# Second product of the expert paths: the last path's rounded rows packed beside their remainder, 14 products a tile for 15

## What is computed

```python
x_mixed = _mix(x, mix_kernel)
h = jnp.einsum('bsd,pdm->bspm', x_mixed, W1) + b1            # 9 paths, 64 wide each
stacked_paths = jnp.einsum('bspm,pmd->bspd', h, W2) + b2     # back to 256
scores = jnp.tanh(x_mixed @ Wo1 + bo1) @ Wo2 + bo2
weights = jax.nn.one_hot(jnp.argmax(scores, axis=-1), 9)
collapsed = jnp.einsum('bspd,bsp->bsd', stacked_paths, weights)
return _layernorm(x + collapsed, gamma, beta)
```

## Time and profile before

| what | us |
|---|---|
| median of three runs | 334.41 (333.69 to 335.15) |
| the profiled execution, its own time | 333.89 |
| its span, first to last instruction | 332.1 |

### The profile page before, as it was taken

The page is one execution under the profiler, slowest core; times in us unless marked ns, Lnnn a source line. Parts: engine busy times, 40 slices in busy tenths (PEclk is TensorE's granted clock), DMA queues, the critical chain, the costliest instruction groups (busy, mean ns, idle before and its releaser), DMA issues. The chain is left out here.

```text
span 332.1 us, 7164 instructions
## 1 busy us (share of the span) xinstructions
PE 301.6 (91%) x2764; PEld 227.6 (69%) x2764; DVE 265.0 (80%) x612; ACT 182.1 (55%) x282; POOL 218.5 (66%) x259
## 2 busy tenths in 40 slices
PE   1687899789999999999999999999999999999991
PEld 1564376365668767796779766796779677967890
DVE  2776799998779796989789796989399768695876
ACT  1364906734971677547852777357553655266620
POOL 0292065683296499966996499957886598629454
PEclk9999779999999999999999999999999999999996
DMA  8952020020002001200120010000100010001003
GB/s 227 221 106 80 2 79 3 0 82 0 3 12 69 2 0 65 80 2 3 65 73 8 0 54 14 1 2 0 65 2 1 3 64 2 2 0 65 0 3 126
DMA packets 20588, 13.16 MB, mean 40 GB/s; under 512 B 10114, under 2 KB 20427, under 8 KB 20555
## 3 DMA queue, kind: packets, MB, share of 16 engines
q1 hardware_dynamic: 18914, 12.14, 12.7%
q10 hardware_dynamic: 1640, 0.57, 0.8%
HBM read 8.51 MB, written 4.19 MB: 38 GB/s over the span
## 5 line engine op out<-in xcount | busy, mean ns | idle before, releaser
L1521 POOL TENSOR_TENSOR rs<-ve,halfneg 128x4 f32<-128x4 f32 x22 | 23.7, 1075 | 43.8 <-DVE ve L1164 43.8
L907 ACT ACTIVATE e<-ps 128x1024 f32<-128x1024 f32 x32 | 31.1, 1024 | 14.1 <-PE ps L584 14.1
L1201 DVE TENSOR_REDUCE mx<-ps 128x16 f32<-128x1024 f32 x32 | 38.0, 1216 | 0.3 <-PE ps L547 0.3
L1615 POOL TENSOR_TENSOR hml<-hs,hmh 128x512 fp32r<-128x512 f32 x28 | 35.0, 1280 | 4.4 <-ACT hmh L969 4.4
L709 PE MATMUL ps<-w2h,hmh 128*128 128x256 f32 (+1 forms) x140 | 35.0, 288 | 0.0
L710 PE MATMUL ps<-w2l,hmh 128*128 128x256 f32 (+1 forms) x140 | 34.1, 280 | 0.0
L620 PE MATMUL ps<-wo,osb 128*128 128x256 f32 x128 | 32.4, 400 | 0.2 <-DVE osb L1228 0.2
L1321 DVE TENSOR_TENSOR hs<-hs,ps 128x512 f32<-128x512 f32 x28 | 18.5, 682 | 16.6 <-PE ps L689 16.6
L1580 POOL TENSOR_TENSOR y<-xh2f,gms 128x256 f32<-128x256 f32 x24 | 20.4, 880 | 16.2 <-DVE xh2f L1173 16.2
L1546 POOL TENSOR_TENSOR x<-xin,bos 128x256 f32<-128x256 f32 x32 | 22.8, 745 | 11.0 <-DVE rDs L1219 10.3
L932 ACT ACTIVATE xh<-x,vb,rs 128x256 f32<-128x256 f32 x22 | 11.5, 591 | 31.5 <-POOL vb L1534 31.5
(11 more groups left out here) (174 smaller groups left out, 800.3 us busy)
## 6 DMA issues: line engine op xcount, KB each, us to landing
xin<-in_x SPq DMA_DIRECT2D x8, 512.0 KB, 3.9
out<-y SPq DMA_DIRECT2D x6, 512.0 KB, 2.9
min_<-in_mask_Bx1xSxS_ik SPq DMA_DIRECT2D x8, 128.0 KB, 3.9
hs<-in_L_ffn_W SPq DMA_DIRECT2D x2, 288.0 KB
hs<-in_L_ffn_W SPq DMA_DIRECT2D x1, 512.0 KB
out<-y SPq DMA_DIRECT2D x2, 256.0 KB, 2.1
out<-xin SPq DMA_DIRECT2D x2, 256.0 KB, 2.3
cst<-in_constants SPq DMA_DIRECT2D x1, 384.0 KB, 6.3
```

The costliest lines, as they stand in the source:

```text
L907: nc.scalar.activation(e[:, 2 * i:2 * i + 2, :], ps[:, bank:bank + 2, :], ACT.Exp).then_inc(s_e, 1)
L1201: v.tensor_reduce(mx[:, k, :].rearrange("p (a h) -> p a h", a=2), ps[:, bank:bank + 2, :].rearrange("p a (h s) -> p a h s", s=SK), AX.X, A ...
L1521: g.tensor_tensor(ln[7][:, :], ln[6][:, :], halfneg[:, :], ALU.pow).then_inc(s_r, 1)
L1615: g.tensor_tensor(L.lo(m, r), L.selected(m, r), L.hi(m, r).bitcast(F32), ALU.subtract).then_inc(L.s_hl, 1)
```

## The change

`m` = 4 is packed differently. The rounded rows of path 8 (64 partitions) are written a second time, to the 64 partitions below the remainder (`hi_below`, on ACT), and `w2h` carries W2[8] twice, one below the other. The one product lo x w2h of m = 4 then uses all 128 partitions and gives lo x w2h plus hi x w2h, so that hi x w2h of its own (L709 for m = 4) falls away: 14 products a tile. b2 leaves `w2h`; its rounded part and its remainder stand one below the other in `w2l` (18 rows below path 8's 64), and the one-hot row is written twice side by side, so that `rep(4)` makes 18 rows of it instead of 64. The setup loads W2[8] and b2 twice and makes b2's two parts with two DVE operations; a memset of `oh` goes.

```diff
-        oh = sb("oh", [P, NT, DM], BF16)
+        oh = sb("oh", [P, NT, 2 * NPATH], BF16)
...
+            def hi_below(self):
+                return hml[DM:, NM - 1, :]
...
         def rows_of(m):
-            return P if m < 4 else DM + NPATH
+            return P if m < 4 else DM + 2 * NPATH
+        def lo_rows_of(m):
+            return P if m < 4 else DM
...
                 load(w2_32[0:DM, 4, :], W2[8], s_wf)
-                load(w2_32[DM:DM + NPATH, 4, :], b2, s_wf)
+                load(w2_32[DM:, 4, :], W2[8], s_wf)
+                for i in range(2):
+                    load(y[DM + i * NPATH:DM + (i + 1) * NPATH, 1, :], b2, s_wf)
...
-                            mm = nc.tensor.matmul(o[DM:, ks], oh[:, k, :], ident_b,
-                                                  start=True, stop=True)
+                            mm = nc.tensor.matmul(o[DM:DM + 2 * NPATH, ks], oh[:, k, :], ident_b, start=True, stop=True)
...
-                        nc.tensor.matmul(o, L.hi(m, r)[:, ks], w2h[0:r, m, :], start=(m == 0), stop=False)
+                        if m < 4:
+                            nc.tensor.matmul(o, L.hi(m, r)[:, ks], w2h[:, m, :], start=(m == 0), stop=False)
                         nc.tensor.matmul(o, L.hi(m, r)[:, ks], w2l[0:r, m, :], start=False, stop=False)
                     else:
                         if k == 0:
                             pe.wait_ge(L.s_hl, L.first + L.count(b, j, NM, m + 1))
-                        mm = nc.tensor.matmul(o, L.lo(m, r)[:, ks], w2h[0:r, m, :], start=False, stop=(m == NM - 1))
+                            if m == NM - 1:
+                                pe.wait_ge(L.s_hb, L.count(b, j, 1, 1))
+                        mm = nc.tensor.matmul(o, L.lo(m, P)[:, ks], w2h[:, m, :], start=False, stop=(m == NM - 1))
...
                 nc.scalar.activation(L.hi(m, r), L.selected(m, r), ACT.Copy).then_inc(L.s_hh, 1)
+                if m == NM - 1:
+                    nc.scalar.activation(L.hi_below(), L.selected(m, DM), ACT.Copy).then_inc(L.s_hb, 1)
...
-                v.memset(oh[:, :, :], 0.0)
...
-                v.tensor_tensor(w2l[0:r, 4, :], w2_32[0:r, 4, :], w2h[0:r, 4, :].bitcast(F32),
-                                ALU.subtract).then_inc(s_w2l, 1)
+                v.tensor_tensor(w2l[0:DM, 4, :], w2_32[0:DM, 4, :], w2h[0:DM, 4, :].bitcast(F32), ALU.subtract)
+                b2_parts = w2l[DM:DM + 2 * NPATH, 4, :]
+                v.tensor_copy(b2_parts, b2_32).then_inc(s_b2h, 1)
+                dve.wait_ge(s_b2h, 1)
+                v.scalar_tensor_tensor(out=b2_parts, in0=b2_parts.bitcast(F32), scalar=cst[DM:DM + 2 * NPATH, C_LB:C_LB + 1],
+                                       in1=b2_32, op0=ALU.mult, op1=ALU.add).then_inc(s_w2l, 1)
...
-                v.tensor_tensor(oh[:, :, 0:NPATH], iota, per_tile(gidx), ALU.is_equal).then_inc(s_oh, 1)
+                twice = [P, NT, 2, NPATH]
+                v.tensor_tensor(oh[:, :, :].rearrange("p k (a n) -> p k a n", a=2),
+                                cst[:, C_IO:C_IO + NPATH].rearrange("p (k a n) -> p k a n", k=1, a=1).broadcast_to(twice),
+                                gidx[:, :].rearrange("p (k a n) -> p k a n", a=1, n=1).broadcast_to(twice),
+                                ALU.is_equal).then_inc(s_oh, 1)
```

More of the change, by code:

```diff
@@ L58 @@
 C_LO = C_IO + NPATH
-C_CST = C_LO + 1
+C_LB = C_LO + 1
+C_CST = C_LB + 1
 C_BC = C_CST
@@ L92, in constants @@
     c[:, C_LO:C_LO + 1] = np.where(r % 32 < 16, 0, -1)
+    c[:, C_LB:C_LB + 1] = np.where(r < DM + NPATH, 0, -1)
     c[:, C_IO:C_IO + NPATH] = np.arange(NPATH) - NPATH
@@ L190, in layer_program @@
         bc32 = y[:, 0, :].rearrange("p (c n) -> p c n", c=KD)
+        b2_32 = y[DM:DM + 2 * NPATH, 1, :]
         ps = stack.enter_context(nc.psum_tensor("ps", [P, 8, CH], F32))
@@ L247, in layer_program @@
         s_lf, s_lfa, s_lfv = sem("last_ffn_filled"), sem("last_ffn_read_by_act"), sem("last_ffn_read_by_dve")
+        s_hb, s_lhb, s_b2h = sem("last_path_hi_below_lo"), sem("last_chunk_last_path_hi_below_lo"), sem("b2_hi")
         s_lhh, s_lhl, s_lones = sem("last_selected_hi"), sem("last_selected_lo"), sem("last_b2_selector_ones")
@@ L283, in layer_program, with __init__ @@
         class Path:
-            def __init__(self, filled, read_by_act, read_by_dve, hi_done, lo_done):
+            def __init__(self, filled, read_by_act, read_by_dve, hi_done, lo_done, hi_below):
                 self.s_f, self.s_fa, self.s_fv, self.s_hh, self.s_hl = filled, read_by_act, read_by_dve, hi_done, lo_done
+                self.s_hb = hi_below
             def filled(self, b, j, use):
@@ L356, in lo, with hi_below @@
                 return qr[0:r, m, :] if m < KD else lhl[0:r, m - KD, :] if m < 4 else xTl[0:r, 0, :]
+            def hi_below(self):
+                return xTl[DM:, 0, :]
             def x(self, k):
@@ L362, in x @@
                 return ps[:, self.banks[("w2a", "w2b", "w2c")[group]], i * D:(i + 1) * D]
-        usual, last = Usual(s_f, s_fa, s_fv, s_hh, s_hl), Last(s_lf, s_lfa, s_lfv, s_lhh, s_lhl)
-        behind = BehindSteps(s_f, s_fa, s_fv, s_hh, s_hl)
+        usual, last = Usual(s_f, s_fa, s_fv, s_hh, s_hl, s_hb), Last(s_lf, s_lfa, s_lfv, s_lhh, s_lhl, s_lhb)
+        behind = BehindSteps(s_f, s_fa, s_fv, s_hh, s_hl, s_hb)
         last_y = xin[:, 1]
         def rows_of(m):
-            return P if m < 4 else DM + NPATH
+            return P if m < 4 else DM + 2 * NPATH
+        def lo_rows_of(m):
+            return P if m < 4 else DM
         block = stack.enter_context(nc.Block())
@@ L866, in split_ffn_weights @@
                 nc.scalar.activation(w2h[:, 0:4, :], w2_32[:, 0:4, :], ACT.Copy)
-                r = DM + NPATH
-                nc.scalar.activation(w2h[0:r, 4, :], w2_32[0:r, 4, :], ACT.Copy).then_inc(s_w2h, 1)
+                nc.scalar.activation(w2h[:, 4, :], w2_32[:, 4, :], ACT.Copy).then_inc(s_w2h, 1)
             def mask_copy(b, j, mask_bank):
@@ L1324, in last_selected_lo @@
             def last_selected_lo(b, j, m):
-                r = rows_of(m)
+                r = lo_rows_of(m)
                 dve.wait_ge(s_lhh, m + 1)
@@ L1699 @@
 WK_LOADS = 4
-WF_LOADS = KD + 1 + 4 + 3 + 4
+WF_LOADS = KD + 1 + 6 + 3 + 4
 _PREFIX = ("L0_xattn_", "L0_ffn_")
```

## The result

| | before | after |
|---|---|---|
| time, median of 4 runs | 334.77 us (333.69 to 335.15) | 338.44 us (336.87 to 339.32) |
| profiled execution, own time | 333.89 us | 338.51 us |
| its span | 332.1 us | 336.7 us |

The ratio of the times is 1.011, with a 95% interval of 1.0064 to 1.0155: slower by 1.1%, 3.7 us between the medians. The forecast was 338.0. The two profiled executions stand 4.6 us apart, a little more than the medians, and these 4.6 are what the traces have to account for.

A forecast was written before the change was run, and what follows sets the result against it. PE was taken to bound the kernel from about 75 us on. `rep(4)` +7.4 and removed products -3.8 gave +3.6 us: 333.89 profiled became 337.5, plus 0.5 for the median 338.0, range 335.8 to 340.6.

The forecast's parts named there:

- What bounds the kernel: From about 75 us to the end PE sets the time; an edit counts by its effect on distances between PE starts.
- The removal: In the w2 tiles, one 256-column product fewer a tile: 32 x 0.119 = 3.8 us less on PE.
- The cover at L631: PE's wait for the second layer norm: 0.86 us of cover before the change, still 0.5 after it.
- The 0.12 that DVE was said to have in hand: DVE's multiplication for m = 4 started 0.12 us after the last mask product, so the chain is later by only 0.81.
- 8 steps of 0.16: In `rep(4)`, alternating widths make eight steps, 1.28 us for 0.35: 0.93 more a chunk, 7.4 us in all.
- The estimate from the 128 cycles: In `rep(4)`, a drain of about 0.053 us a switch: a step of 0.11, 4.6 us in all, sum +0.8.
- Copy, remainder, setup: Added work on ACT, POOL and DVE's setup, and loads on SP: all hidden; uncovered, the copy would cost 0.63 a chunk.
- the copy delay ACT's L959 by about 0.1: In the tail, the copy delays L959 by about 0.1 us, hidden because `rep(4)` makes PE later by 0.93.
- The sum: Whole kernel: +7.4 - 3.8 = +3.6 us, with ends of +1.4 and +6.2.
- The two widths pass each other: Rival: in `rep(4)` the two widths run side by side without a switch, it stays at 0.35, 330.6 us; chance 0.12.
- A light switch: Rival: in `rep(4)` alternating costs half a switch, a step of 0.11, sum +0.4, 334.8 us; chance 0.07.
- The layer norm chain: Rival: the chain grows beyond its 0.5 cover, PE waits at L631 in five steps, 2 us more, 340.0; chance 0.08.

The follow-up runs named there:

- e1: The changed kernel with the second product of `rep(4)` made 36 columns wide instead of 18; 332.06 us, 0.9935 of before.
- e2: The changed kernel with that second product 64 columns wide and the memset of `oh` in setup again; 331.90 us, 0.9922 of before.
- e3: The changed kernel with `rep(4)` reordered, the four 64-wide products first, then the four 18-wide; 334.28 us, 0.9992 of before.
- e7: The changed kernel with `rep(4)` ordered 64, 18, 18, 64, 64, 18, 18, 64; 336.88 us, 1.0083 of before.
- e4: The kernel before with only the second half of `rep(4)` cut to 18 columns, 15 products a tile kept; 342.0 us, 1.0218 of before.
- e6: e2 with ACT's copy for chunk 7 moved behind the hidden rows of chunk 8 in the tail; 331.24 us, 0.9910 of before.
- e8: e6 with `scores_for_max(front, 2)` issued ahead of `rep(3)` instead of between `rep(3)` and `rep(4)`; 331.22 us, 0.9897 of before.
- e11: The changed kernel with one tiny one-column memset more on DVE in setup; 338.91 us (2 runs), 1.0128 of before.
- e5: e1 with the copy on ACT issued twice, the second waiting for the first; 332.4 us, 0.9940 of before.

## Why the prediction was right, and where it was not

- **What bounds the kernel**: PE's distance between starts, held. Every edit's worth could be read off the chunk: 0.48 predicted as 0.45.
- **The removal**, 0.119 us a product, 3.8 in all: right in the steady chunks (e1: 0.49 a chunk) and in the last w2 section. The full 3.8 never reached the end in a kernel without the narrow product: e2 has 2.65. The step that was too optimistic is the cover at L631: 0.86 was read from one steady chunk, the last step has none, and there the whole 0.48 of the gain goes. In the kernel after this hardly mattered, since `rep(4)` gave PE more time than was removed.
- **The cover at L631 in the steady chunk**, 0.5 foretold: measured 0.38 (ACT ends at 111.46, L650 starts at 111.84). The 0.12 that DVE was said to have in hand is not in hand. Its multiplication for m = 4 starts 0.11 behind the end of the masks in the kernel after too (102.56 behind 102.45), so the whole delay went into the chain and the cover shrank by the whole 0.48 of the removal.
- **`rep(4)`**, 8 steps of 0.16, 1.28 us: measured 1.30, with steps of 0.172 and 0.154. e3 and e7 show that most of it goes with the number of changes, at 0.10 to 0.11 each, and e4 that it is the width alone. The rule of the Trainium skill, TensorEngine Tiling (Array Packing), Key Properties, is that a change of tiling mode drains the engine. These traces agree in that every change has its price, also between two parts that share no column; that the price is a drain they do not show. The estimate from the 128 cycles of the Trainium skill, TensorE: Matmul & The Clock Gate, Step-by-step: what each phase is for (a step of 0.11, sum +0.8), was too low: the rows' 0.09 to 0.12 were the better source.
- **Copy, remainder, setup**: hidden in the steady chunks and in DVE's setup, as said; the loads ahead of 28 us are not decided. DVE's idle time ahead of its first reciprocal was 1.32 and is 0.77 with the added work. In the tail I had the copy delay ACT's L959 by about 0.1, and PE later by 0.93. The first was too little: ACT has two activations to do there before PE can go on, and only PE's own delay hides the copy. With a cheap `rep(4)` it costs 0.28 (e2 against e6).
- **The sum**, +3.6: the medians differ by 3.67, the profiled executions by 4.6. Of the further 1.0 of the profiled pair 0.6 is the long chunk, which no row of before could show, 0.12 the last step, whose waits I had not looked at, and 0.2 is `rep(4)` itself, 1.30 for 1.28 us in each chunk. The mechanism and its size were foretold; that the medians meet the forecast to 0.1 us is partly luck, since their interval runs from 2.1 to 5.2 us.
- **The rivals.** *The two widths pass each other* is refuted by the eight rows of `rep(4)`. For this rival the Trainium skill's page TensorE: Matmul & The Clock Gate, Part 3, spoke (concurrent products on different tile positions); in the traces that holds for 64 columns beside 64 (0.01 apart in the earlier trace rows) and for 36 beside 64 (e1), and not for 18 beside 64. *A light switch* (0.11 a step) is refuted by 0.154 and more. *The layer norm chain* did not decide here, but it does in e2's last step and in the steady chunks of e8. The condition that I gave, that something in the chain grows, holds for e8, where the chain grew by 0.33; in e2's last step it was not needed, since there PE's own work shrank below a chain that stayed as it was.

## What to carry to other kernels

On TensorE look at the shape of the array's part that each product uses, in the order of issue: every change cost 0.10 to 0.12 us here, nearly as much as a whole 256-column product (0.119), and a narrower product between wider ones can cost more than it saves, as it did here. Pad it until it runs beside its neighbours (36 columns did as well as 64), or group the shapes. And when work is taken from the engine that bounds, read the cover of its waits in every kind of stage, the last one and the tail too, not in one steady chunk: 0.86 us in one place was nothing in another.

## What had not been expected of the hardware

- A step from the 64-wide to the 18-column product is longer than the one back, 0.172 for 0.154 us, in after and in e4 alike. That goes with the product that the step starts from, and not with the direction: where a second product of the same shape has come before the change, the step is 0.149 either way (e7), and the first product of a shape, whose weight load starts with it, shows 0.243 us against 0.219 later when 64 wide and 0.224 when 18 wide. The 0.024 and 0.005 more are what the two steps have above 0.149.
- The four 64-wide products on one half of the array take 0.34 us with their step to the next shape (e3), and four pairs on both halves take 0.35 to L620: the second product of a pair is free, as long as no change of the part lies between (64 beside 64, and 36 beside 64 in e1).
- DVE can lose 0.4 us at one place of a long program, and one instruction more in its setup removes that (after, e11). A chunk that is longer than its like is worth a look before it is put down to the change.
- Setup differs between profiled executions more than most edits here are worth. Its end, the third start of `negmax_transposed`, lies between 71.4 us (e8) and 75.1 (e6). A part is there by the first start already, 27.8 (e8) to 29.3 (e6); the rest goes with the granted clock. From 30 to 74 us it is 1.00 in e1, e8 and after, 0.92 in before and 0.88 in e5 and e6, and the stretch from the first start to the third takes 43.6 us in the first three, 44.3 in before and 45.8 in the last two. From 74 us to behind the last matmuls all these kernels stand at 1.00 (after: 74 to 330 us). Between kernels that differ by less than 1 us the chunk and the tail decide, not the whole span.
